# Two graph layers on one core: layer 0's product table as four tables, ring places by one load of four registers, and tails zeroed over chunks 1 to 25

## The reference

```python
s1 = jnp.einsum('ea,eb,abc->ec', xs, es, W1) * k1      # 64 columns
s2 = jnp.einsum('eai,ebi,abc->ec', xv, ev, W2) * k2    # 64 columns, the same as s1's
v1 = jnp.einsum('ea,ebi,abc->eci', xs, ev, W3) * k3    # 32 x 3 columns
v2 = jnp.einsum('eai,eb,abc->eci', xv, es, W4) * k4    # 32 x 3 columns
messages = concatenate([(s1 + s2), (v1 + v2)]) @ Wm + bm
agg = segment_sum(messages, row, N_NODES)
upd = concatenate([x, agg], -1) @ Wu + bu
x = layernorm(x + x + upd)
```

## Time and profile before

| | us |
|---|---|
| median of 3 runs | 3240.68 (3239.31 to 3241.97) |
| the profiled execution | 3242.32 |
| its span, first to last instruction | 3240.5 |

### The profile page before, as it was taken

How to read it: one execution, slowest core, us unless ns; L and a number is a source line. 1 busy time by engine, 2 the same in 40 slices (tenths; PEclk the granted TensorE clock), 3 DMA queues, 4 the chain that set the end, 5 groups by cost and what they waited for, 6 DMA issues and landing times. The chain is left out here.

```text
span 3240.5 us, 57553 instructions
## 1 busy us (share of the span) xinstructions
PE 2745.7 (85%) x16776; PEld 2456.1 (76%) x16776; DVE 1967.2 (61%) x5263; ACT 722.1 (22%) x2123; POOL 1663.9 (51%) x1771
## 2 busy tenths in 40 slices
PE   2699999999999999879997687777777787778877
PEld 1587778887888888769996677777777777777777
DVE  7367666666666676458776455555555555555555
ACT  1232233323322333112221111111111111111111
POOL 1365565665656666611111656555566555656553
PEclk7899999999999999989998788988888888888898
DMA  8899999999999999568884422222222222222221
GB/s 302 272 310 302 276 311 299 296 300 304 303 310 302 307 298 299 183 224 288 295 280 163 128 69 68 69 68 78 67 70 70 76 69 66 70 80 68 69 67 53
DMA packets 452374, 609.94 MB, mean 188 GB/s; under 512 B 81687, under 2 KB 378345, under 8 KB 439482
## 3 DMA queue, kind: packets, MB, share of 16 engines
q10 hardware_dynamic: 237795, 282.85, 27.3%
q1 hardware_dynamic: 130104, 174.19, 17.1%
q0 software_dynamic: 84176, 149.08, 15.8%
HBM read 377.76 MB, written 228.11 MB: 187 GB/s over the span
## 5 line engine op out<-in xcount | busy, mean ns | idle before, releaser
L1415 POOL DMA_INDIRECT f_y<-y_table,b_rec x894 | 853.7, 955 | 597.6 <-DVE f_msg L1479 323.7
L442 POOL DMA_INDIRECT placed<-message,slots_now x784 | 765.8, 977 | 574.1 <-ACT message L601 376.1
L524 PE MATMUL g_bank<-quad_ring,front_work 128*128 x6272 | 961.0, 305 | 72.7 <-DMA quad_ring<-products 44.3
L524 PEld LDWEIGHTS g_bank<-quad_ring,front_work 128*128 128x128 f32 x6272 | 881.1, 191 | 180.6 <-issue 177.5
L1476 DVE TENSOR_TENSOR f_msg<-e_bank,f_y 128x256 f32<-128x256 f32 x447 | 186.6, 417 | 648.3 <-remote 361.0
L760 DVE SCALAR_TENSOR_TENSOR front_work<-g_bank,quarter_node,front_work 128x512 f32<-128x512 f32 x784 | 529.1, 742 | 72.1 <-PE g_bank L501 59.0
L1605 PE MATMUL e_bank<-f_msg,f_hot 128*126 128x160 f32 x1788 | 416.5, 329 | 70.9 <-issue 39.2
L1600 PE MATMUL e_bank<-f_msg,f_hot 128*126 128x160 f32 x1788 | 428.7, 322 | 22.7 <-issue 22.5
L1588 PE MATMUL e_bank<-fc,b_hidden 100*128 100x192 f32 x1788 | 421.5, 363 | 0.4 <-issue 0.4
L1605 PEld LDWEIGHTS e_bank<-f_msg,f_hot 128*126 128x126 f32 x1788 | 321.9, 209 | 92.0 <-issue 49.0
L1600 PEld LDWEIGHTS e_bank<-f_msg,f_hot 128*126 128x126 f32 x1788 | 329.2, 208 | 30.9 <-issue 30.7
(11 more groups left out here) (237 smaller groups left out, 2538.8 us busy)
## 6 DMA issues: line engine op xcount, KB each, us to landing
products<-g ACTq DMA_DIRECT2D x49, 2560.0 KB
quad_ring<-products ACTq DMA_DIRECT2D x98, 1280.0 KB
big<-placed SPq DMA_DIRECT2D x49, 1458.0 KB, 6.9
front_work<-in_e_t SPq DMA_DIRECT2D x784, 64.0 KB
b_lengths<-length_parts ACTq DMA_DIRECT2D x447, 45.0 KB
f_y<-y_table,b_rec POOLq DMA_INDIRECT x894
placed<-message,slots_now POOLq DMA_INDIRECT x784
placed<-zeros SPq DMA_DIRECT2D x1, 8100.0 KB, 31.8
```

The costliest lines, as they stand in the source:

```text
L442: pool.indirect_dma_start(v.placed[:, :], bass.IndirectOffsetOnAxis(slots_now[tile // SET % SLOT_SETS][:, tile % SET:tile % SET + 1], 0), ...
L524: last = pe.matmul(bank_now[:, n * D:n * D + D], spread[batch % SPREADS][:, j, q * P:q * P + P], ring[:, bass.ds(slot + j, 1), :].rearrang ...
L1415: pool.indirect_dma_start(f_y[:, tile % Y_RING, :], None, v.y_table[:, :], bass.IndirectOffsetOnAxis(b_rec[b % REC_RING][:, j, 0:1], 0)).t ...
```

## The change

1. **Four tables.** The table's 32 rows a node are kept in four tables, of 8 rows each (the scalars b, and the three directions), of 160, 96, 96 and 128 columns. The columns are put in an order in which the 64 scalar columns stand beside each direction's 32. A block is 3,840 instead of 5,120 numbers a node. It is written with four transfers. A unit is loaded with four, each onto a quarter of the partitions: 32 partitions x 16 rows of 640, 384, 384 or 512 bytes; the wrap-around quads take four instead of one. The columns of the ring that no table fills are zeroed once, on POOL.
2. **Edge numbers.** Partitions of the ring are now (table, node, row) instead of (node, row). So each of a batch's four loads of edge numbers takes 8 rows, four times over: the source is a pattern of 4 repeats x 8 rows, the destination 32 partitions as before, 64 KB as before.
3. **Places.** One load of four registers a batch brings the four tiles' ring places; the shifts, masks and packing are gone.
4. **Tails.** The zeros of `placed` are written in 25 transfers of 2 blocks, one a chunk in chunks 1 to 25 behind the chunk's first batch. POOL waits for them at tile 464 (chunk 29). One count of how many rows each block had by then is kept and checked at the end.
5. **Opening.** Ring units 0 and 1 are loaded before block 2's parts are taken, units 2 and 3 after.

The fallback paths for other edge orders change in the same way, and are not run here.

```diff
-GW = NB * D
+TABLES = ((0, 160, 0), (1280, 96, 0), (2048, 96, 32), (2816, 128, 32))
+GW = 3840
...
-                        sp.dma_start(features[h][32 * n:32 * n + 32, :, :].rearrange("p a b -> p (a b)"), t["e32_t"][:, edges]).then_inc(edges_in[h], 16)
+                        sp.dma_start(features[h][32 * n:32 * n + 32, :, :].rearrange("p a b -> p (a b)"),
+                                     t["e32_t"][8 * n:8 * n + 8, edges].unsqueeze(0).broadcast_to([4, 8, 4 * P])).then_inc(edges_in[h], 16)
...
-                clear(0, FAST_BLOCKS // 2)
                 load_x(2)
-                sp.wait_ge(tables_out, 48)
+                sp.wait_ge(tables_out, 32)
                 for batch in range(4):
                     load_batch(batch)
-                clear(FAST_BLOCKS // 2, FAST_BLOCKS)
...
+                        if h == 0 and 1 <= c <= CLEAR_PIECES:
+                            clear((c - 1) * CLEARED_AT_ONCE, min(c * CLEARED_AT_ONCE, FAST_BLOCKS))
...
+                    if tile == TAILS_CLEAR * CHUNK:
+                        pool.wait_ge(cleared, 16 * CLEAR_PIECES)
...
-                pool.wait_ge(cleared, 32)
...
-                        slot = nc.s_assert_within((words[batch] >> (8 * q)) & 127, 0, RING_QUADS - 1)
+                        slot = places[batch][q]
...
-                        act.dma_start(v.products[b * P:b * P + P, :], into[:].rearrange("p b d -> p (b d)")).then_inc(g_out[b % 2], 16)
+                        for table, (at, w, _) in zip(v.products, TABLES):
+                            act.dma_start(table[b * P:b * P + P, :], into[:, at:at + 8 * w]).then_inc(g_out[b % 2], 16)
...
-                    quads = v.products.rearrange("(g n) (b c) -> (n b) g c", n=4, b=NB)
-                    act.dma_start(ring[:, at:at + UNIT, :], quads[:, u * UNIT:u * UNIT + UNIT, :]).then_inc(quads_in[u % RING], 16)
-                    if u % RING == 0:
-                        act.dma_start(ring[:, RING_QUADS:, :], quads[:, u * UNIT:u * UNIT + WRAP, :]).then_inc(quads_in[0], 16)
+                    for n, (table, (_, w, first)) in enumerate(zip(v.products, TABLES)):
+                        quads = table.rearrange("(g n) (b c) -> (n b) g c", n=4, b=8)
+                        into = ring[32 * n:32 * n + 32, :, first:first + w]
+                        act.dma_start(into[:, at:at + UNIT, :], quads[:, u * UNIT:u * UNIT + UNIT, :]).then_inc(quads_in[u % RING], 16)
+                        if u % RING == 0:
+                            act.dma_start(into[:, RING_QUADS:, :], quads[:, u * UNIT:u * UNIT + WRAP, :]).then_inc(quads_in[0], 16)
```

## The result

The changed kernel takes 3349.3 us (median of 4 runs, 3344.6 to 3361.7), the kernel before in the same session 3241.3 us (3239.3 to 3245.7). The ratio is 1.034 [1.031, 1.037]: slower, by 108 us. The forecast was 3378 us. In the profiled execution, of 3346.9 us with a span of 3345.2, L535 is the line of the loop's matmuls that was L524; L486 was L476, L511 was L501, L585 was L570, L617 and L619 were L599 and L601, L607 and L609 were L589 and L591.

A forecast was written before the change was run, and what follows sets the result against it. Two limits a few per cent apart were seen: TensorE with its register instructions, and the 16 DMA engines. Loop +174, opening -40, checks +1 gave +135 us on 3242.3 profiled; forecast 3378 us, range 3280 to 3520.

The forecast's parts named there:

- The edge numbers: Loop: each load of edge numbers runs on four of 16 DMA engines, which become the limit; loop +174 us, chance 0.70.
- The sum per chunk: Loop: work on each of the four engines, 31.2 us (32.9 with zeros), divided by 1.08: 28.9 and 30.5 us a chunk.
- the divisor for overlapping packets: Loop: packet times overlap, so the engines' sums are divided by something between 1 and 1.11; 1.08 taken.
- The opening: Before the loop: without the zeros ahead, the loop starts near 66 us instead of 106.67; -40 us (-55 to -20).
- four stores for one add 3 issues of 0.37 us: Opening, block 2's parts: writing four tables instead of one costs only three more issues of 0.37 us each.
- costs nothing: Opening: POOL zeroes the ring's unused columns before its small stores at 24 us; needed only at 66, so free.
- The zeros: Chunks 1 to 25: the moved zeros cost 1.7 us a chunk, hidden only as far as engines have time left.
- the rival with 16 engines: Loop: edge numbers stay on 16 engines, TensorE is the limit and gains 46 us; 3156 us (3120 to 3200), chance 0.21.
- The registers: Loop, TensorE: removing 1,686 ALU instructions gains 1.0 us a chunk (0.67 to 2.8), only where nothing else limits.
- ScalarE's issues: Loop, rival: more ring-load issues hold ScalarE, 0.75 us excess twice a chunk, +74 us; 3275 us with 16 engines, chance 0.06.
- Short rows: Loop, rival: 384-byte ring rows take twice the line's 31.8 ns, +109 us; 3311 us with 16 engines, chance 0.03.
- over 40 ns: Loop: q10's time per packet above this would show that short ring rows cost extra, the rival with chance 0.03.

The follow-up runs named there:

- e1: The changed kernel with edge numbers handed over as 128 rows, each load taking 32 plain rows on 16 engines; 3265.8 us, 0.991 of the kernel before.
- e2: The kernel before, its edge numbers laid in memory as 4 groups of 8 rows with gaps, so loads use 4 engines; 3479.4 us, ratio 1.057.
- e3: The kernel before, its edge numbers laid in memory as 8 groups of 4 rows with gaps, so loads use 8 engines; 3341.9 us, ratio 1.016.
- e4: The kernel before, its edge numbers in 16 groups of 2 rows with gaps, the control on 16 engines; 3326.1 us, ratio 1.010.
- e11: e8 with the ring's first four units also issued by SP, so all ring loads are; 3242.5 us, 0.984 of the kernel before.
- e6: The kernel before with only the zeros moved, from two transfers ahead of the loop to 25 pieces in chunks 1 to 25; 3288.8 us, ratio 0.998.
- e7: e1 with the zeros back ahead of the loop in two transfers; 3275.3 us, 0.995 of the kernel before.
- e5: The kernel before with only the ring places changed, one load of four registers replacing the shifted and masked word; 3266.9 us, ratio 0.993.
- e10: e8 with a batch's ring places again taken from one word by shift and mask; 3261.7 us, 0.991 of the kernel before.
- e8: e1 with the loop's ring loads issued by SP instead of ScalarE; 3251.9 us, 0.986 of the kernel before.
- e12: e11 with one load of 128 rows for a batch's edge numbers instead of four of 32; 2832.9 us against 2887.3 before, ratio 0.981.

## Why the prediction was right, and where it was not

**The edge numbers: right in kind and nearly in size.** Four engines by the packets of q1, +4.1% by e1 and +4.7% by e2. That the same four are used each time has the ring's lateness for it, the few moments with more than four rows under way although SP issues four loads in a row, and the rule of the Trainium skill that the prediction cited (DMA: Bandwidth & Descriptors, "Why a DMA increments its semaphore by 16 and not by 1"); q1's packets in e2, e3 and e4 agree with that rule's numbers of engines, 4, 8 and 16; that they are the lowest-numbered ones no run here can show.

**The sum per chunk: 3% too long.** I had 30.5 us with zeros and 28.9 without; measured 29.8 and 28.1. The term at fault is the divisor for overlapping packets, 1.08 chosen; the earlier trace rows had shown 1.11. With 1.11 the sums are 29.6 and 28.1. The packets' own times give 12.1 us for the loads on each of the four (13.0 taken) and 19.0 for everything else (18.2 taken): two errors that offset each other, so the sum of 31.2 was right partly by luck. For e2 the same terms (13.0 for its loads, 21.0 for the unchanged table, ring and messages) give 34.0 / 1.11 = 30.6, measured 30.8; its packets say 33.1 and a divisor of 1.08, so the divisor is good to some 3%. The loop came out at 1404 us instead of 1446.

**The opening: half of it.** -22 instead of -40. The step that failed is "four stores for one add 3 issues of 0.37 us". Twelve issues stood between block 1 and block 2 on ScalarE's queue, because the change also moved the loads of units 0 and 1 ahead of block 2's copies, and these issues took 0.5 to 1.9 us each, with 6.0 for the last four. I had costed the stores' issues and not these. With all 16 engines the loop starts at 75.7, with the issues on SP at 68.9: 9 us for the four engines, 7 for ScalarE's issues. A second step failed as well: POOL's zeroing of the ring "costs nothing". VectorE lost 6 us beside it between 18 and 25 us, so the counts came 5.5 us late and block 2's parts began at 49.5 instead of some 43.6, in the change and in e11 alike. That e11 starts only 3 us after my 66 is thus partly luck: the rest, from the start of the parts to the loop, took 20 us there instead of my 22. No run moves the zeroing, so what it is worth in the end is not shown; the counts' 5.5 us are the most that this trace allows.

**The zeros: right here, wrong for the other case.** The chunks with zeros are 1.7 us longer, as written. In the rival with 16 engines I let them vanish in a share of 0.91; e6 shows them cost 25 us at a share of 0.98, e7 and e1 16 us at 0.93 (110 to 700 us each).

**The registers: below my lower bound.** 0.33 us a chunk in e5 and 0.35 in e10, against 1.0 taken and 0.67 as the lower end. That end was all of TensorE's idle time; it was no lower bound, since most of this idle time belongs to other things and is still there. In the changed kernel the gain can't be seen, since TensorE, busy 91% of the loop, is not the limit there.

**The rivals.** *16 engines*: its sum, 3156 or 0.974, is refuted even where its condition holds (e1, 0.991); it counted 46 us for the registers, and it left ScalarE free. *ScalarE's issues*: refuted as the main cause, but present: 8.7 us of hold a chunk in the change and 6.8 in e1. Moving them away is worth 0.5 to 0.7% (e8, e11), 16 to 23 us, where I had priced them at 74. I had treated it as a case of its own, while it lies on top of either other one. *Short rows*: refuted. From 200 to 1200 us q10 took 48.1% of 16,000 us over 171,131 packets = 45 ns each, below the 59 ns before (62.8%, 170,588). The prediction's sign for this rival, "over 40 ns", was set wrong: 40 ns is a ring row's time, while q10's mean holds the table's long rows too, and the main case's own 13.5 us a chunk and engine, over the 4,989 packets a chunk that came, is 43. By size, from 600 to 900 us, the trace has 28 ns on the mean for a packet of 384 bytes, 33 for 512 and 41 for 640.

The two errors, 42 us too long in the loop and 18 us too early in the opening, partly cancel: 3378 against 3349, inside the stated 3280 to 3520.

## What to carry to other kernels

Before a DMA's access pattern is rewritten, count how many engines its outer dimension lets it use: the same bytes in rows of the same size ran on 4 engines instead of 16, and that cost more than all the rest of the change could give; completion packets per transfer show it, and a mean DMA share that falls while transfers come late is the sign. One transfer split into four is four issues on its engine's queue, so give them to an engine with nothing else to do and look at what stands behind them in the opening. And look at what a newly added instruction of an idle engine runs beside: here it slowed another engine's small ones.

## What the runs showed of the hardware that I had not expected

- The same kernel takes 3241, 3291 and 2887 us on different chips, with a narrow spread on each (3239 to 3246, 3283 to 3305, 2882 to 2890); only ratios against the kernel before on the same chip, or microseconds of one stage, can be compared. Behind the front phase, from 2000 to 2600 us, the granted clock was 0.87 in e11 and 0.99 in e12.
- A plain load with 16 groups of two rows and a gap row between them costs 0.95% of the kernel more than one of 32 adjacent rows, with the same number of packets (38,994 on q1 for 586 loads, by the sum above 38,670 at 48 a load). The cause stays open.
- The packets' times of two busy queues add up to 1.11 of the engines' time, and on four full engines the packets' times add up to 1.11 of the time in the change and 1.08 in e2.
- One load of four registers (327 ns at least, 138 in the stretch) instead of one word, a fused operation and some 11 shifts and masks a batch saved only 0.33 us a chunk, so nearly all of them ran beside matmuls.
- While POOL zeroed 32 x 2,656 numbers (2.3 us), a VectorE instruction on 49 x 16 numbers took 2.3 us instead of 0.17, three times in a row; VectorE's reductions of 2.27 us beside POOL's first one kept their time.
